# Three GIN layers of a graph network on one core: the last 448 nodes summed by gathered rows instead of a dense product

## The reference, cut to what matters

```python
def _gin_layer(x, src, dst, W, b):
    agg = jax.ops.segment_sum(x[src], dst, num_segments=N_NODES)
    h = (x + agg) @ W.T + b
    return jax.nn.relu(h)
```

## Time and profile before

| | us |
|---|---|
| Median of 3 runs | 3326.15 (3320.41 to 3328.97) |
| The profiled execution's own time | 3324.86 |
| Its span, first to last instruction | 3323.1 |
| TensorE busy (matmul) | 3010.9 (91%) |
| VectorE, ScalarE, GpSimd busy | 1521.2, 903.9, 979.6 |
| Mean granted TensorE clock | 0.936 |
| DMA | 796.32 MB, 240 GB/s over the span |

### The profile page before, as it was taken

One profiled execution on the slowest core, in us unless ns is written; L12 is line 12 of the kernel. 1 busy time (PEld: TensorE's weight loads), 2 busy tenths in 40 slices (PEclk: granted clock), 3 DMA queues, 4 the chain that ended last, 5 costly groups with the idle time before them and its releaser, 6 DMA issues.

```text
span 3323.1 us, 75539 instructions
## 1 busy us (share of the span) xinstructions
PE 3010.9 (91%) x29405; PEld 1917.6 (58%) x29405; DVE 1521.2 (46%) x4507; ACT 903.9 (27%) x2115; POOL 979.6 (29%) x1210
## 2 busy tenths in 40 slices
PE   6999999999999887878789787878889999999998
PEld 5888888888888533434345343434445555555554
DVE  7888888888887233324332243434432001001111
ACT  5666666666665100000001000101022001001111
POOL 3222222222223344555541364564520000000000
PEclk7999999999999988878889887888889999999999
DMA  5655565656532866657576565756655876886885
GB/s 190 266 228 247 223 248 224 247 223 249 223 125 87 331 236 234 244 198 272 185 273 267 217 247 180 272 202 236 240 222 217 305 301 262 305 304 261 299 308 188
DMA packets 149997, 796.32 MB, mean 240 GB/s; under 512 B 19172, under 2 KB 29352, under 8 KB 136072
## 3 DMA queue, kind: packets, MB, share of 16 engines
q1 hardware_dynamic: 119960, 729.87, 55.9%
q0 software_dynamic: 27216, 54.53, 5.6%
q10 hardware_dynamic: 2720, 10.62, 0.8%
HBM read 567.98 MB, written 226.97 MB: 239 GB/s over the span
## 4 chain that ended last, share of the span: by engine, by line
PE 90%; issue 8%; DVE 1%; ACT 0%; DMA 0%; POOL 0%; another core or an unknown queue 0%; ACTq 0%; DVEq 0%; POOLq 0%
PE ps L928 28%; PE ps L1132 23%; PE ps L1211 18%; PE ps L1204 11%; PE ps L938 2%; PE ps L939 2%; PE ps L1224 1%; PE ps L940 1%; PE ps L941 1%; PE ps L1225 1%; PE ps L1111 1%; PE ps L1226 0%; PE ps L1227 0%; PE ps L1078 0%; PE ps L1100 0%
## 5 line engine op out<-in xcount | busy, mean ns | idle before, releaser
L928 PE MATMUL ps<-ring,Y 128*128 128x448 f32 x2352 | 949.8, 557 | 198.7 <-issue 198.6
L841 POOL DMA_INDIRECT ring<-y_rows,ring x700 | 675.3, 965 | 699.6 <-DVE ring L1744 436.9
L928 PEld LDWEIGHTS ps<-ring,Y 128*128 128x128 f32 x2352 | 456.8, 195 | 674.0 <-issue 674.0
L1132 PE MATMUL ps<-ring,Y 128*128 128x448 f16 x4116 | 780.6, 352 | 0.0
L1608 ACT ACTIVATE ring<-ps 128x392 f16<-128x392 f32 (+1 forms) x1568 | 653.8, 504 | 307.7 <-PE ps L1204 299.1
L1132 PEld LDWEIGHTS ps<-ring,Y 128*128 128x128 f16 x4116 | 402.7, 98 | 373.8
L1211 PE MATMUL ps<-ring,Y 128*128 (+1 forms) x2744 | 614.0, 366 | 3.3 <-issue 2.8
L1744 DVE SCALAR_TENSOR_TENSOR ring<-ring 128x128 f32<-128x128 f32 x1384 | 404.5, 347 | 381.1 <-DMA ring<-y_rows,ring 210.1
L1211 PEld LDWEIGHTS ps<-ring,Y 128*128 128x128 f32 x2744 | 490.5, 189 | 19.4 <-issue 4.0
L1204 PEld LDWEIGHTS ps<-shared 64*128 64x128 bf16 x18816 | 342.2, 94 | 135.4 <-ACT ring L1608 88.7
L1204 PE MATMUL ps<-shared 64*128 64x49 bf16 (+1 forms) x18816 | 392.9, 191 | 24.3 <-issue 12.5
(11 more groups left out here) (190 smaller groups left out, 1303.9 us busy)
## 6 DMA issues: line engine op xcount, KB each, us to landing
ring<-adj_w SPq DMA_DIRECT2D x72, 2688.0 KB
adj_w<-ring SPq DMA_DIRECT2D x48, 2744.0 KB, 12.2
ring<-adj_h SPq DMA_DIRECT2D x42, 2800.0 KB, 9.5
ring<-adj_h SPq DMA_DIRECT2D x42, 2688.0 KB, 9.2
adj_h<-ring SPq DMA_DIRECT2D x56, 1372.0 KB, 5.0
ring<-adj_w SPq DMA_DIRECT2D x24, 2912.0 KB
ring<-y_rows,ring POOLq DMA_INDIRECT x700
y_rows<-Y ACTq DMA_DIRECT2D x2, 2560.0 KB, 10.8
```

Of the source, the lines that this page charges most:

```text
L841: pool.indirect_dma_start(out=run_rows[:, i % ROW_BUFS, :], out_offset=None, in_=y_rows, in_offset=bass.IndirectOffsetOnAxis(ap=run_edges[ ...
L928: mm = pe.matmul(ps[:, bank, 0:GW], Y[:, h, :], slab(s)[:, :, h - h0, :], start=(h == 0), stop=(last and h == TILES - 1))
L1132: mm = pe.matmul(ps[:, par, 0:GW], part[:, h, :], counts_slab(par, s)[:, :, h - h0, :], start=(h == 0 and part is Y_high), stop=(h == TILE ...
```

## The change

Group 13 of each count layer (nodes 5,824 to 6,271) is no longer a dense product. Its 224 windows of two nodes are cut into three lists: 32 windows in four quarters of 25 edges each (the quarters on 32 lanes each), 128 windows with 100 edges, and 64 windows in two halves of 50. That makes 25 + 100 + 50 = 175 rounds, each one indirect DMA of 128 rows of 512 bytes (256 f16 values: the high and the low part side by side, for which Y_high and Y_low are interleaved by tile).

- GpSimd prepares the quarters' lists and fold matrices between the two GRU layers' gathers (prepare_picks), and in each count layer stores Y to y_rows in two DMAs (28 tiles, then 21) as soon as it is complete, then issues the 175 gathers into a ring of nine buffers (fetch_picks).
- VectorE makes masks of 0 and 1 in place of weights (mark_picks, six instructions) and adds the rows: 350 adds of 256 elements per layer (add_picks), in twelve portions behind the groups 0 to 11, in the last layer in six portions, each ahead of a pair's finish. Its loops are written out. It and ScalarE wait for the stores of y_rows before they overwrite Y in the next layer.
- TensorE runs 13 groups. Between the halves of group 12 it adds the nodes' own values (own_terms, 16 small f16 matmuls) and flips the first two lists; in the last layer the flips of pair five follow there. Behind the second half it flips the third list (12 fp32 matmuls in all per layer), ScalarE rectifies group 13 (rectify_rows), and the last pair's seven tiles are flipped back behind that.
- SP no longer requests group 13. The next layer's group 0 waits for the release of group 12's halves (the extra term "first"), and group 1 by its count for the same.
- In the last layer ScalarE's finish of pair five stands ahead of the rectification of groups 12 and 13.

```diff
+COUNT_GROUPS = GROUPS - 1
+ROWS_FROM = COUNT_GROUPS * GW
+SPLIT = 4
+QUARTER = RUN // SPLIT
+PICK_LANES = P // SPLIT
+PICK_LENGTHS = [QUARTER, RUN_LENGTHS[2], RUN_LENGTHS[3]]
+PICK_STARTS = [0, QUARTER, QUARTER + RUN_LENGTHS[2]]
+PICKS = len(PICK_LENGTHS)
+PICK_ROUNDS = sum(PICK_LENGTHS)
+PICK_BUFS = 9
+KEPT_FIRST = 28
...
-        Y_high = y_flat[:, 0:NODES // 2].bitcast(F16).rearrange("p (t f) -> p t f", f=P)
-        Y_low = y_flat[:, NODES // 2:NODES].bitcast(F16).rearrange("p (t f) -> p t f", f=P)
+        Y_parts = y_flat.bitcast(F16).rearrange("p (t k f) -> p t k f", k=2, f=P)
+        Y_high, Y_low = Y_parts[:, :, 0, :], Y_parts[:, :, 1, :]
...
+        select = [fold_quarters, ident[:, :], fold_halves]
...
-                    sp.wait_ge(s_used_h, HALVES * (GROUPS * l + 2 * i + r) + s + 1)
+                    first = HALVES if l and isinstance(i, int) and i == r == 0 else 0
+                    sp.wait_ge(s_used_h, HALVES * (COUNT_GROUPS * l + 2 * i + r) + first + s + 1)
...
+                    for r in range(2 if l else 0):
+                        for s in range(HALVES):
+                            stream_counts(l, 0, r, s)
+                    with sp.Fori(1 if l else 2, PAIRS - 1) as i:
                         for r in range(2):
                             for s in range(HALVES):
                                 stream_counts(l, i, r, s)
+                    for s in range(HALVES):
+                        stream_counts(l, PAIRS - 1, 0, s)
                 for i in range(PAIRS):
-                    for r in range(2):
+                    for r in range(2 if i < PAIRS - 1 else 1):
                         for s in range(HALVES):
                             stream_counts(N_LAYERS - 1, i, r, s)
                     if i >= 2:
...
+            def prepare_picks():
...
+                for q in range(SPLIT):
+                    pool.dma_start(quarter_edges[q * PICK_LANES:(q + 1) * PICK_LANES, :, :],
+                                   run_edges[P - PICK_LANES:P, RUN_STARTS[1] + q * QUARTER:RUN_STARTS[1] + (q + 1) * QUARTER, :])\
+                        .then_inc(s_pickl, 16)
+            def fetch_picks(l):
+                pool.wait_ge(s_acc, WIN * pick_base(l))
+                if l == 0:
+                    pool.wait_ge(s_flipr, 2 * (N_LAYERS - 1))
+                    pool.wait_ge(s_pickl, 16 * SPLIT)
+                rows = y_rows.rearrange("(p t) f -> p t f", t=TILES)
+                pool.wait_ge(s_ye1, START + (y_base(l, TILES) + KEPT_FIRST // CHUNK if l else KEPT_FIRST))
+                pool.dma_start(rows[:, 0:KEPT_FIRST, :], Y[:, 0:KEPT_FIRST, :]).then_inc(s_yrows, 16)
+                pool.wait_ge(s_ye1, START + (y_base(l, TILES) + NC if l else TILES))
+                pool.dma_start(rows[:, KEPT_FIRST:TILES, :], Y[:, KEPT_FIRST:TILES, :]).then_inc(s_yrows, 16)
+                pool.wait_ge(s_yrows, 32 * (l + 1))
+                for i in range(PICK_ROUNDS):
+                    if i >= PICK_BUFS:
+                        pool.wait_ge(s_acc, WIN * (pick_base(l) + i - PICK_BUFS + 1))
+                    pool.indirect_dma_start(out=pick_rows[:, i % PICK_BUFS, :], out_offset=None, in_=y_rows,
+                                            in_offset=bass.IndirectOffsetOnAxis(ap=pick_source(i).bitcast(I32), axis=0))\
+                        .then_inc(s_prow[i % PICK_BUFS], 16)
...
-                for layer in range(N_LAYERS - 1):
-                    fetch_rows(layer)
+                fetch_rows(0)
+                prepare_picks()
+                fetch_rows(1)
+                for l in range(N_LAYERS):
+                    fetch_picks(l)
...
+            def own_terms(l):
+                pe.wait_ge(s_act, (l + 1) * GROUPS)
+                if l == 0:
+                    pe.wait_ge(s_picks, SPLIT + 3)
+                for t in range(ROWS_FROM // P, TILES):
+                    r0 = max(0, ROWS_FROM - t * P)
+                    w0, n = (t * P + r0 - ROWS_FROM) // WIN, (P - r0) // WIN
+                    for d in range(WIN):
+                        c = d * GW // WIN + w0
+                        for part in (Y_high, Y_low):
+                            pe.matmul(ps[:, 1, c:c + n], part[:, t, :],
+                                      ident_h.rearrange("p (w d) -> p d w", d=WIN)[:, d, r0 // WIN:P // WIN],
+                                      start=(t == ROWS_FROM // P and d == 0 and part is Y_high), stop=False)
+            def flip_picks(l, lists):
+                for k in lists:
+                    pe.wait_ge(s_acc, WIN * (pick_base(l) + PICK_STARTS[k] + PICK_LENGTHS[k]))
+                    n, w0 = [(PICK_LANES, 0), (P, PICK_LANES), (P // 2, PICK_LANES + P)][k]
+                    for d in range(WIN):
+                        c = d * GW // WIN + w0
+                        for half in range(2):
+                            mm = pe.matmul(ps[:, 1, c:c + n], pick_sums[:, k, d, half * P:(half + 1) * P], select[k][:, 0:n],
+                                           start=False, stop=(k == PICKS - 1 and d == WIN - 1 and half == 1))
+                    if k == PICKS - 1:
+                        mm.then_inc(s_flipc, 1)
+            def last_groups(l):
+                i = PAIRS - 1
+                pe.wait_ge(s_act, l * GROUPS + 2 * i + 1)
+                halves_of_group(l, i, 0, (0,))
+                own_terms(l)
+                flip_picks(l, range(2))
+                if l == N_LAYERS - 1:
+                    for c in range(2):
+                        flip_out(PAIRS - 2, c)
+                halves_of_group(l, i, 0, (1,))
...
-                    with pe.Fori(1, PAIRS) as i:
+                    with pe.Fori(1, PAIRS - 1) as i:
                         for par in range(2):
                             count_group(l, i, par)
+                    last_groups(l)
+                    flip_picks(l, range(2, PICKS))
                 l = N_LAYERS - 1
                 messages(l)
-                for i in range(PAIRS):
+                for i in range(PAIRS - 1):
                     count_group(l, i, 0, fresh=(i == 0))
                     if i:
                         for c in range(2):
                             flip_out(i - 1, c)
-                    if i < PAIRS - 1:
-                        count_group(l, i, 1)
-                    else:
-                        pe.wait_ge(s_act, l * GROUPS + 2 * i + 2)
-                        halves_of_group(l, i, 1, (0,))
-                        flip_out(i, 0)
-                        halves_of_group(l, i, 1, (1,))
-                        flip_out(i, 1)
+                    count_group(l, i, 1)
+                last_groups(l)
+                flip_picks(l, range(2, PICKS))
+                for c in range(2):
+                    flip_out(PAIRS - 1, c)
...
+            def rectify_rows(l):
+                act.wait_ge(s_flipc, l + 1)
+                act.activation(group(xT, GROUPS - 1).rearrange("p (w d) -> p d w", d=WIN),
+                               ps[:, 1, 0:GW].rearrange("p (d w) -> p d w", d=WIN), ACT.Relu, bias=bcur[:, 0:1],
                                scale=unscale[:, 0:1].bitcast(F32)).then_inc(s_act, 1)
...
-                rectify(l, PAIRS - 1, 0)
                 for c in range(2):
                     finish(PAIRS - 2, c)
+                rectify(l, PAIRS - 1, 0)
+                rectify_rows(l)
                 finish(PAIRS - 1, 0)
-                rectify(l, PAIRS - 1, 1)
                 finish(PAIRS - 1, 1, k_end=LAST_ACT)
...
+            def add_picks(l, lo, hi):
+                for i in range(lo, hi):
+                    k, r = pick_of(i)
+                    buf, done = i % PICK_BUFS, WIN * (pick_base(l) + i)
+                    dve.wait_ge(s_prow[buf], 16 * (len(range(buf, PICK_ROUNDS, PICK_BUFS)) * l + i // PICK_BUFS + 1))
+                    if r == 0 and l:
+                        dve.wait_ge(s_flipc, l)
+                    for d in range(WIN):
+                        if r:
+                            dve.wait_ge(s_acc, done + d + 1 - WIN)
+                            add = dve.scalar_tensor_tensor(out=pick_sums[:, k, d, :], in0=pick_halves[:, buf, :],
+                                                           scalar=pick_mask(i, d), in1=pick_sums[:, k, d, :],
+                                                           op0=ALU.mult, op1=ALU.add)
+                        else:
+                            add = dve.tensor_scalar(pick_sums[:, k, d, :], pick_halves[:, buf, :], pick_mask(i, d), None, ALU.mult)
+                        add.then_inc(s_acc, 1)
...
+                        dve.wait_ge(s_yrows, 32 * l)
...
-                        with dve.Fori(0, GROUPS) as g:
+                        for g in range(GROUPS):
                             dve.wait_ge(s_act, FREE + l * GROUPS + g + 1)
-                            dve.sem_inc(s_mark, 1)
-                            dve.tensor_reduce(x_tops[:, bass.ds(g, 1)], group(xT, g), mybir.AxisListType.X, ALU.max)\
```

(23 more changed lines are left out.)

64 lines of the change are left out of this document (62 added, 2 removed).

## The result

The changed kernel took 3632.05 us (median of 4 runs, 3618.45 to 3649.75), the kernel before 3323.28 beside it (3314.36 to 3328.97): ratio 1.0933, 95% interval 1.0905 to 1.0961, 309 us slower. Forecast was 3379, and the range ended at 3405: the direction was right, the size far off.

A forecast was written before the change was run, and what follows sets the result against it. TensorE's f16 matmuls were taken to bound the count layers. Layer effects of +22, +1 and +25 us and 6 for the clock sum to 54: 3324.9 + 54 = 3379, range 3294 to 3405.

The forecast's parts named there:

- Removed work, own terms and flips, tail: Count layers: group 13's products save 18.54 us each; own terms and flips add 3.5 each, the last layer's tail 4.
- Covers: VectorE in count layers: adds of 0.40 us, 175 rounds in 140 us, hidden beside 225 us of dense groups.
- Gathers 1.25 us apart: GpSimd in count layers: 175 gathers, 0.94 us each and 1.25 apart, take 219 us per layer.
- sum 30: Gain over the three count layers with no further effect: 6, 14 and 10 us, giving 3295.
- Rival B: Count layers: slow stretches don't come with f16 pairs; 3295, or 3306 with gathers 0.03 us further apart; chance 0.27.
- DMA is enough: Count layers: stream at 303 GB/s plus gathers at 52 make 355, within the 420 GB/s the engines move.
- rival C: Count layers: DMA is the limit, the stream falling behind by 0.5 us a group; 3313, chance 0.07.
- I take the rule: stream silent, gathers alone, 5 us: Late in each count layer, that state drops TensorE to a pair per 2.8 us; 84 us, forecast chance 0.58.
- Bounds: Count layers: slow pair of 1.2 us gives +16; onset at 3.5 us or gathers 4 us later, +66 to +80.
- Clock: Count layers: granted clock at its lower level by each slow stretch's end and shortly after; 2 us each, 6.

The follow-up runs named there:

- experiment 15: Kernel before plus unread GpSimd DMAs per count layer (ordinary; 64-row gathers; 128-row gathers each with a waited fill), on a chip that starves: 3593.32 us.
- experiment 1: Changed kernel with three gather rounds per count layer in place of 175, the other gathers and adds left out: 3271.21 us, ratio 0.9853.
- 6: Kernel before, GpSimd waiting for the landing of every eighth gather of the GRU layers: 3210.34 us, ratio 0.9727.
- 8: Changed kernel, GpSimd waiting for the landing of every eighth gather of the count layers: 3476.49 us, ratio 1.0528.
- 3: Kernel before plus unread GpSimd work in the count layers (150 gathers back to back; 150 with waits at each eighth; 150 fills): 3517.58 us.
- experiment 13: Kernel before with 450 additional unread GpSimd transfers in the count layers, a repeat on the fourth chip, where nothing starves: 2945.5 us.
- experiment 12: Changed kernel without edit on the fourth chip, where nothing starves: 2952.77 us against 2944.68, ratio 1.0022.

## Why the prediction was wrong, step by step

- **Removed work, own terms and flips, tail**: right, and a little dear. 55.6 us; 3.2 a layer for 3.5. All that isn't a gather costs 8 to 10, where the sum had 10.5 + 4.
- **Covers**: VectorE's add is 0.480 us, for 0.40 (worked out from adds of f32; these read f16). Two are 0.96 a round and still shorter than a gather, so no term of its own, but see the next.
- **Gathers 1.25 us apart**: mis-sized. 1.33 to 1.43 where nothing starves, 231 to 250 us a layer for 219. The gathers themselves last longer, 1.05 us in the mean for 0.94, beside VectorE's adds. The pauses between them are hardly longer: most of the 90.9 us of idle time before L945 put down to VectorE is the usual 0.30 each time, and only once did the ring hold GpSimd up for longer than 1 us (5.02, at 2737.96). Layers 1 and 2 were said to be covered by 6 us. This turns most of the "sum 30" of the effects without a slow state into nothing (1.0022, with 42.8 us of late sums). Rival B named this case ("GpSimd slower than 1.25") but priced only 0.03 us more.
- **DMA is enough**: right. 419 GB/s with TensorE at 54 pairs per 10 us in experiment 15. The Trainium skill's figure of about 358 ("DMA: Bandwidth & Descriptors", "Where 436 GB/s comes from") doesn't bind here; rival C is out.
- **"I take the rule: stream silent, gathers alone, 5 us"**: the step that failed. The stretches it was read from the earlier trace rows all have a silent stream, but that isn't what begins them. In the GRU layers the stream had filled its slabs some 5 us earlier (60 GB/s from 1288 on, with TensorE still full), by coincidence; TensorE, once slow, frees no slab, and that keeps it silent. In the count layers it went on to move 405 GB/s through the drop. What begins a stretch is the run of gathers: with them away (experiment 1) or broken up (6, 8) it doesn't come, and unread ones bring it (3). The row that told was at hand. The stretch before the one of the earlier trace rows, in the kernel before, from GpSimd's first gather of the group on:

```profile
1264.80:1292.80 28.00, 28.00 (x75) 14.07 (x75) 16.20 (x58) 0.00 (x0) 21.48 (x22) 1.00 0.83 314
1292.80:1310.00 17.20, 5.32 (x8) 1.62 (x6) 2.02 (x6) 0.00 (x0) 10.38 (x11) 0.61 0.18 46
```

75 pairs after 22 gathers, and in the other GRU groups 68 to 78; 80 to 86 with the quicker f16 pairs at each layer's start. Nearly the same number of pairs after 28 and after 16 us, 22 and 13 gathers: nearer to a count of TensorE's instructions than to a time. It isn't a strict one. Most later runs in the count layers drop after 14 to 16 gathers and 117 to 134 pairs; their second gather was held up for some 6 us, in which 30 pairs fit. So the ring's first fill begins a stretch at once and most later runs of 14 or more gathers begin others: 15 stretches, not three, and 352.6 us where I had priced 84. The direction came out right because stretches did come, not because they came where and when the rule has them.
- **Bounds**: they varied the length of three stretches and never their number, so the range ended 227 us below the median. Two slips of the sum, 2.6 for half of 5.6 and 22 for 2788 - 2765, change nothing.
- **Clock**: 0.50 to 0.57 over a stretch, as said, a small part.
- **Rival B**'s condition (no issue gaps in the count layers) holds on the fourth chip, and not for its reason: no gaps in the GRU layers either. Even there its 3295, 30 us below the kernel before, didn't come.

## What to carry to other kernels

If an engine slows down now and then, line up all the stretches on when another engine *began* something, and count instructions as well as us, before making a rule of what is silent beside it: what has stopped by then may be a coincidence, and stay so as a result. Gathers put on GpSimd beside dense work have a price that doesn't show at low counts: here three rounds gained 47.5 us, 87 gained nothing and 175 lost 309. On chips that starve, GpSimd waiting in the kernel before for one landing in 16 gathers (ratio 0.9633) or 8 (0.9727) gains 93 to 117 us, three times what the forecast gave the change without slow stretches (30). Where nothing starves, waits at each twelfth (or at each eighth, for the gather before it) cost 6%. No version with a wait ran on both kinds of chip, so none is shown to be good everywhere: time a change on more than one.

## What the runs showed of the hardware that I had not expected

- Chips differ: the same kernel took 3303 to 3325 us on three and 2944.7 and 2944.8 on two others, 358 of 379 us of it in the GRU layers with their runs of gathers. Why wasn't found.
- On the three, gathers issued by GpSimd 0.30 us after each other leave TensorE some 68 to 86 pairs, then one instruction per 1.4 us, even with nobody reading the rows, until 2 to 5 us after the last, in two cases 21 and 27. Ordinary DMAs and fills on GpSimd don't do it.
- The mechanism stays open. That TensorE lives on instructions fetched ahead, and GpSimd's work for a gather holds up the fetching, fits the runs but is argued, not shown. The DMA packets of instructions in the trace don't bear it out. In 490 us of the second GRU layer, with nine stretches, these are all packets by queue (packets, MB, share of 16 engines):

```profile
q1 hardware_dynamic: 16898, 89.92, 47.0%
q0 software_dynamic: 8983, 18.39, 12.8%
q14 instruction: 9, 0.07, 0.0%
```

Nine packets of instructions, then; in the same loop of experiment 13, where nothing starves, there are eight. If fetching is held up, it is on a path that the trace doesn't show.

- Some gathers that meet a run of VectorE's f16 adds took up to 6.4 us instead of 0.95, till that run ended; in experiment 12 ten of 525 took over 1.5 us.
